# A six-sublayer network in one program: seams joined, a first unit issued ahead, the value bias folded away

## What is computed

```
x = x + 0.5 * ffn(_layernorm(x))      # 8 routed experts, top 2, and a shared one of width 1024
x = x + attn(_layernorm(x))           # gated linear attention, 4 heads, chunks of 16
x = x + 0.5 * ffn(_layernorm(x))      # the same experts again
x = x + 0.5 * ffn1(_layernorm(x))     # ternary weights, relu, width 1024
x = x + local(_layernorm(x))          # 16 heads of 16, window of 33 tokens
x = x + 0.5 * ffn1(_layernorm(x))
```

## Time and profile before

| what | value |
|---|---|
| time, median of 3 runs | 1747.06 us |
| lowest and highest | 1745.62 and 1749.57 us |
| profiled execution: time | 1750.36 us |
| its span, mean granted clock of TensorE | 1748.3 us, 0.984 |
| busy: PE, DVE, ACT, POOL | 94%, 65%, 49%, 39% |
| stages in the profile, us from the start of the span | first `ffn0` to 467, `gla` to 797, second `ffn0` to 1249, `l1ffn` to 1383, `win` to 1624, `l1ffn` to the end |

### The profile page before, as it was taken

The page is one execution under the profiler, slowest core; times in us unless marked ns, Lnnn a source line. Parts: engine busy times, 40 slices in busy tenths (PEclk is TensorE's granted clock), DMA queues, the critical chain, the costliest instruction groups (busy, mean ns, idle before and its releaser), DMA issues.

```text
span 1748.3 us, 42002 instructions
## 1 busy us (share of the span) xinstructions
PE 1650.5 (94%) x14972; PEld 1109.8 (63%) x14973; DVE 1142.2 (65%) x2498; ACT 857.5 (49%) x1475; POOL 682.4 (39%) x655
## 2 busy tenths in 40 slices
PE   6999999999989999989899999999799979998999
PEld 3565656666567767665555656666466657776666
DVE  6677766666466666657765556665577477777675
ACT  4355434443466566644344334443366455664764
POOL 2342323443122222132333324433244587887243
PEclk9999999999989999999999999999899999998999
DMA  7132323332211111003210123332332033131011
GB/s 251 49 108 83 106 74 103 109 111 91 52 38 36 24 24 24 1 1 94 85 38 34 39 67 111 110 112 83 80 67 42 1 75 74 40 76 39 14 36 48
DMA packets 90149, 115.82 MB, mean 66 GB/s; under 512 B 9296, under 2 KB 76400, under 8 KB 90032
## 3 DMA queue, kind: packets, MB, share of 16 engines
q1 hardware_dynamic: 68624, 70.25, 14.5%
q0 software_dynamic: 21408, 43.93, 9.0%
HBM read 66.24 MB, written 47.90 MB: 65 GB/s over the span
## 4 chain that ended last, share of the span: by engine, by line
PE 57%; DVE 6%; POOL 4%; ACT 3%; issue 2%; DMA 0%; DVEq 0%; SPq 0%; ACTq 0%; POOLq 0%
PE ps L1675 10%; PE ps L1677 10%; PE ps L1676 10%; PE ps L1909 3%; PE ps L1908 3%; PE ps L1691 2%; PE ps L2006 2%; PE ps L1890 2%; PE ps L1891 2%; PE ps L2163 2%; PE ps L2145 1%; PE ps L2011 1%; PE ps L2133 1%; POOL work L746 1%; PE ps L1970 1%
## 5 line engine op out<-in xcount | busy, mean ns | idle before, releaser
L703 POOL DMA_INDIRECT routed<-work x142 | 136.1, 959 | 234.9 <-DVE work L1431 229.8
L1675 PE MATMUL ps<-later_hi,work 128*128 (+1 forms) x632 | 203.2, 322 | 1.2 <-ACT work L1044 1.0
L1676 PE MATMUL ps<-later_lo,work 128*128 (+1 forms) x632 | 203.1, 321 | 0.0
L1677 PE MATMUL ps<-later_hi,work 128*128 (+1 forms) x632 | 203.0, 321 | 0.0
L1675 PE MATMUL ps<-xt_hi,wsh 128*128 128x512 f16 x512 | 194.9, 381 | 4.7 <-DVEq L1185 2.2
L1676 PE MATMUL ps<-xt_lo,wsh 128*128 128x512 f16 x512 | 194.9, 381 | 0.0
L1677 PE MATMUL ps<-xt_hi,wsh 128*128 128x512 f16 x512 | 194.8, 380 | 0.0
L640 POOL TENSOR_TENSOR rstd<-mv,eps 128x4 f32<-128x4 f32 x49 | 15.2, 309 | 409.1 <-DVE mv L1140 398.4
L854 ACT ACTIVATE work<-ps 128x512 f32<-128x512 f32 x128 | 76.4, 597 | 181.5 <-PE ps L1677 170.8
L1675 PE MATMUL ps<-wsh,work 128*128 128x256 f16 x512 | 140.7, 275 | 4.8 <-ACT work L843 2.7
L1324 DVE SCALAR_TENSOR_TENSOR work<-ps,work 128x512 f32<-128x512 f32 x128 | 88.1, 689 | 84.4 <-ACT work L854 69.1
(11 more groups left out here) (246 smaller groups left out, 4257.0 us busy)
## 6 DMA issues: line engine op xcount, KB each, us to landing
work<-expert_x SPq DMA_DIRECT2D x142, 129.0 KB
yg<-in_w_later SPq DMA_DIRECT2D x9, 496.0 KB
w1q<-in_w_later SPq DMA_DIRECT2D x9, 496.0 KB
yg<-routed SPq DMA_DIRECT2D x8, 512.0 KB, 3.7
yg<-routed POOLq DMA_DIRECT2D x8, 512.0 KB, 6.0
yg<-in_w SPq DMA_DIRECT2D x8, 512.0 KB
later_hi<-routed SPq DMA_DIRECT2D x8, 512.0 KB, 3.8
later_hi<-routed POOLq DMA_DIRECT2D x8, 512.0 KB, 5.9
```

The lines of the kernel that those rows point to most:

```text
L703: nc.gpsimd.indirect_dma_start(routed[:, :], bass.IndirectOffsetOnAxis(m.homes[:, i:i + 1], 0), m.t_y[:, i % 4, :], None).then_inc(s[f"til ...
L1675: nc.tensor.matmul(out_, a[0], b[0], start=start, stop=False)
L1676: nc.tensor.matmul(out_, a[0], b[1], start=False, stop=False)
L1677: return nc.tensor.matmul(out_, a[1], b[0], start=False, stop=stop)
```

## The change

**Behind the tiles (end of both `ffn0`).** Both routed rows of sequence 0 come by plain DMAs of SP into two free buffers (`opening_buffers`). DVE adds them to x in the middle of the last shared body (`combine_opening`, behind unit 4), and takes the statistics behind unit 6. The other operations of the chain move up too, and sequence 1 is combined and normed there, before the last `take`. PE transposes sequence 0 inside `down(0)`. The l1ffn behind it starts with sequence 1 normed (`AHEAD`), and `TURN_AT` is 4 in place of 2, in both `l1ffn`.

**Linear attention.** Its opening on DVE loses combine, statistics and scale of sequence 1. Its last body issues the first up unit of the next `ffn0` before `turn(0)`; the two pairs of banks of `up_bank` change places.

**Local attention.** The value bias isn't added to the values; since the weights of a softmax sum to 1, its product with the output weights is added to the output bias (`value_bias`, 6 matmuls, and one DVE operation), and the padding rows are filled with its negative. Sequence 1 is normed in the last part of `l1ffn` on DVE, and not by POOL; the two memsets of POOL move into `l1ffn`; the output bias of sequence g is added by POOL in step g. PE opens in another order.

**Elsewhere.** PE waits for `x_updated` before `gla` alone, and inside `l1ffn` before its first transposes. Loads at the start are a little smaller. The core of the diff:

```diff
-TURN_AT = 2
-AHEAD = ("win", )
+TURN_AT = 4
+AHEAD = ("ffn0", "win", )
...
+        def opening_buffers():
+
+            return xn[:, :, 0:D], ffn0_space().tile_x[:, :, 0:D]
...
         def up_bank(g, q):
 
-            return 2 * (q % 3) if is_last(g) else 2 + 2 * (q % 2)
+            return 2 * (q % 3) if is_last(g) else 4 - 2 * (q % 2)
...
+                for r in range(TOPK):
+                    sp.dma_start(opening_buffers()[r], routed_rows(0, r)).then_inc(s["opening"], 16)
                 buffers = yg_buffers(n + 1)
-                for q in range(NSEQ):
-                    if q >= len(buffers):
+                for q in range(1, NSEQ):
+                    if q > len(buffers):
                         sp.wait_ge(s["combined"], q + 1 - len(buffers) + G0)
...
+                    if ahead_of_win(n) and g >= NSEQ - 2:
+                        if g == NSEQ - 1:
+                            pool.wait_ge(S[n - 1]["combined"], 2 * NSEQ)
+                        nc.gpsimd.memset(win_space().vz[NSEQ - 1 - g], 0.0).then_inc(S[n + 1]["zeroed"], 1)
+                if ahead_of_win(n):
+                    rstd_of(N0(n + 1) + 1)
...
-                second_rows(n, 0)
-                rstd_of(N0(n + 1))
                 second_rows(n, 1)
+                for q in range(2):
+                    rstd_of(N0(n + 1) + q)
...
-                    if not is_last(g) and not second_last(g):
-                        output_bias(next_seq(g + 2))
+                    if is_first(g):
+                        pool.wait_ge(s["bias_row"], 1)
+                    output_bias(next_seq(g))
...
-                rstd_of(N0(n) + 1)
-                centre(N0(n) + 1, TPS)
-                scale(N0(n) + 1)
-                for q in range(2):
-                    output_bias(q * TPS)
-                nc.gpsimd.memset(m.vz[0], 0.0)
-                nc.gpsimd.memset(m.vz[1], 0.0).then_inc(s["zeroed"], 1)
...
+                nc.scalar.activation(m.bv[0], bv_col, ACT.Copy).then_inc(s["bias_hi"], 1)
                 queries_keys(0, 0, range(2 * KT))
-                nc.scalar.activation(m.sel[0:33, :], const("rowsel")[0:33, 0:1].broadcast_to([33, P]), ACT.Copy)
-                nc.scalar.activation(m.brow[0:33, :], rows[0:33, 2 * D:4 * D], ACT.Copy, scale=WS).then_inc(s["bias_hi"], 1)
+                xt_hi_of(N0(n) + 1, 1, WXT)
                 values_rows(0)
-                xt_hi_of(N0(n) + 1, 1, WXT)
                 windowed(act, step)
...
+            def combine_opening(n):
+
+                s = S[n]
+                first, second = opening_buffers()
+                dve.wait_ge(s["opening"], 32 * (1 + earlier(n)))
+                nc.vector.tensor_tensor(second, second, first, ALU.add).then_inc(s["opened"], 1)
+                dve.wait_ge(s["opened"], 1 + earlier(n))
+                nc.vector.tensor_tensor(x[:, 0:TPS, :], x[:, 0:TPS, :], second, ALU.add).then_inc(s["combined"], 1)
+                dve.wait_ge(s["combined"], 1 + earlier(n) * NSEQ)
                 dve.sem_inc(stood, 1)
...
+                        if is_last(g) and k == 4:
+                            combine_opening(n)
+                        if is_last(g) and k == 6:
+                            ln_stats(N0(n + 1), 0)
...
-                        combine(n, 0, 0)
-                        ln_stats(N0(n + 1), 0)
+                        ln_scale(N0(n + 1), 0)
+                        combine(n, 1, 1)
+                        ln_stats(N0(n + 1) + 1, TPS)
+                        xt_lo_of(N0(n + 1), 0)
...
                         ln_scale(g + N0(n) + 2, (g + 2) * TPS, into=m.xn[u])
                     take(0)
                     if is_last(g):
-                        ln_scale(N0(n + 1), 0)
-                        xt_lo_of(N0(n + 1), 0)
+                        ln_scale(N0(n + 1) + 1, TPS)
...
+                    if ahead_of_win(n) and is_last(g):
+                        ln_stats(N0(n + 1) + 1, TPS)
...
+                    if ahead_of_win(n) and is_last(g):
+                        ln_scale(N0(n + 1) + 1, TPS)
...
-                combine(n - 1, 1, 1)
-                ln_stats(N0(n) + 1, TPS)
-                ln_scale(N0(n) + 1, TPS)
...
+                        if t == 0 and is_first(g):
+                            ln_stats(N0(n) + 2, 2 * TPS)
+                            dve.wait_ge(s["bias_product"], 1)
+                            nc.vector.scalar_tensor_tensor(out=bo_row, in0=ps[:, 7, 0:D], scalar=1 / WS, in1=bo_row,
+                                                           op0=ALU.mult, op1=ALU.add).then_inc(s["bias_row"], 1)
...
+            def shared_unit(n, g, u, q):
+
+                b = up_bank(g, q)
+                for half in range(2):
+                    for k in range(KT):
+                        w = both((wsh1, wsh2)[half], slice(k * HSH + q * P, k * HSH + (q + 1) * P))
+                        ins = mm3(ps[:, b + half, :], w, xt(u, k), k == 0, k == KT - 1)
+                ins.then_inc(S[n]["up_ready"], 1)
+
+            def unit_ahead(n, g):
+
+                return is_first(g) and n > 0 and SUBLAYERS[n - 1] == "gla"
 
...
-                        up(q)
+                        if q or not unit_ahead(n, g):
+                            up(q)
...
-                        down(0)
-                        transposes(N0(n + 1))
+                        down(0, lambda: transposes(N0(n + 1)))
                         down(1)
...
                         if q == TURN_AT and is_first(g) and normed_ahead(n):
+                            pe.wait_ge(x_updated, N0(n))
                             transposes(N0(n) + 1)
...
+                    elif unit_ahead(n + 1, 0):
+                        xt_ready(N0(n + 1))
+                        gate_left(1)
+                        shared_unit(n + 1, 0, 0, 0)
                     turn(0)
...
-                def bias(half, at):
-                    nc.tensor.matmul(ps[:, half, :], m.sel[0:33, :], m.brow[0:33, None, at:at + D].broadcast_to([33, 2, D]),
-                                     start=True, stop=False, skip_group_check=True)
...
+                def value_bias():
+
+                    pe.wait_ge(s["bias_lo"], 1)
+                    for f in range(KT):
+                        own = tuple(b[:, f:f + 1].broadcast_to([P, P]) for b in m.bv)
+                        ins = mm3(ps[:, 7, 0:D], own, both(ao, slice(f * D, (f + 1) * D)), f == 0, f == KT - 1)
+                    ins.then_inc(s["bias_product"], 1)
...
-                        bias(half, D)
...
-                queries_keys(0, 0, range(2 * KT))
+                queries_keys(0, 0, range(KT))
+                transposes(N0(n) + 1, b=WXT)
+                queries_keys(0, 0, range(KT, 2 * KT))
+                scores(0, 0, 0)
                 values_rows(0, 0)
-                transposes(N0(n) + 1, b=WXT)
-                scores(0, 0, 0)
+                value_bias()
...
-                if n:
+                if kind == "gla":
                     pe.wait_ge(x_updated, N0(n))
```

More of the change, by code:

```diff
@@ L86 @@
 CONST_COLS = {"ident": 128, "ones": 128, "causal": 128, "cumref": 128, "tri": NE * NE,
-              "window": 64, "heads": 2, "heads_ws": 2, "rowsel": 1, "iota": TILES, "regions": NE,
+              "window": 64, "heads": 2, "heads_ws": 2, "iota": TILES, "regions": NE,
               "home": TOPK * NSEQ * TPS, "nowhere": TILES}
@@ L151, in build @@
         w2q = sb("w2q", [P, FU * D], F16)
-        rows = sb("rows", [P, 5 * D + NE])
+        rows = sb("rows", [P, 4 * D + NE])
         bgk_row, b2_row, bo_row = (rows[:, n * D:(n + 1) * D] for n in range(3))
-        bv_row = rows[:, 3 * D:5 * D]
-        ebias_row = rows[:, 5 * D:]
-        cols = sb("cols", [P, FU + 2 * KT + 1])
+        bv_row = rows[:, 3 * D:4 * D]
+        ebias_row = rows[:, 4 * D:]
+        cols = sb("cols", [P, FU + 3 * KT + 1])
         b1_col, bq_col, bk_col = cols[:, 0:FU], cols[:, FU:FU + KT], cols[:, FU + KT:FU + 2 * KT]
-        rms_col = cols[:, FU + 2 * KT:]
+        bv_col = cols[:, FU + 2 * KT:FU + 3 * KT]
+        rms_col = cols[:, FU + 3 * KT:]
         xn = sb("xn", [P, TPS, RW])
@@ L352, in back_by @@
         def back_by(n, q, odd):
-            return 8 * (q - odd) + 16 + 8 * NSEQ * earlier(n)
+            done = 16 * (NSEQ // 2 - (0 if odd else 1)) * earlier(n)
+            return 8 * (q - odd) + (16 if odd else 0) + done
         def yg_buffers(n):
@@ L432, in win_space @@
             m.hb = w([KT, 2])
-            m.brow, m.sel = w([2 * D], F16), w([P], F16)
+            m.bv = w([KT], F16), w([KT], F16)
             m.vrow = w([TPS, D])
@@ L824, in later_hi @@
                     act.wait_ge(ready0, 2)
-                    nc.scalar.activation(go[0][:], later_stage(odd, H * D), ACT.Copy, scale=rms_col).then_inc(later_hi_done, 1)
+                    nc.scalar.activation(go[0][:], later_stage(odd, H * D), ACT.Copy, scale=rms_col).then_inc(w_hi_done, 1)
                 else:
```

(11 more changed lines are left out.)

52 lines of the change are left out of this document (22 added, 30 removed).

## The result

The changed kernel takes 1716.88 us in the median of 4 runs (1716.48 to 1718.23), the kernel before 1747.84 (1745.62 to 1749.57): a ratio of 0.9825, 95% interval 0.9808 to 0.9842. That is 31.0 us less; 36.3 were forecast. Later, on one chip and beside each other, 5 runs gave 1715.97 against 1741.35 in 11 (0.985, 0.9837 to 0.9864), 25.4 us less. On two other chips the kernel before took 1748.57 and 1750.10 us (9 runs each), so it differs by 9 us with the chip. The chip of the first pair isn't on record, so whether 31.0 or 25.4 is nearer to what the change is worth stays open. The profiled execution has a span of 1714.4 us, 33.9 less than that of before, and a mean clock of 0.989.

The account below looks back on a forecast made before the run. PE, busy 94% of the span, was taken to set the time, with seams costing idle time and clock. Seven terms, 3.7 + 3.2 + 3.6 + 12.5 + 9.9 + 4.1 - 0.7, gave 36.3 us: 1710.7 from 1747.06, range 1703 to 1724.

Parts of the forecast that it names:

- First seam: From ffn0 to gla: the wait for the scale goes, transposes and down tile run at the high clock level; 3.7 us.
- Opening of linear attention: Keys' product starts when ACT's exponentials end, 1.85 us, plus half of the 2.76 lost by low clock, 1.35; sum 3.2.
- End of linear attention: A unit of 12 matmuls fills PE's wait before the turns and the x_updated wait goes; 3.6 us, bounds 2.5 and 4.7.
- Behind the second tiles: All four PE waits and the low clock go, less a new wait of 1.7; 12.5 us, bounds 9 and 13.5.
- Opening of local attention: POOL's first subtraction comes earlier, as sequence 1 is already normed; 9.9 us, bounds 8 and 11.
- Value bias: Bias matmuls leave PE's own path in six steps of local attention; 4.1 us, bounds 0 and 5.6.
- Last stage: TURN_AT of 4 loses 1.75 us against 1.05 from the earlier start; -0.7, bounds -1.2 and +0.5.
- seams only half closed: Rival, chance 0.25: VectorE has as much work, only in another order, so the seams give less; gain 27 us, 1720.
- Value bias beside the path: Rival, chance 0.07: the chain maximum, subtraction, exponential sets local attention's steps and covers PE's matmuls; gain 32.2 us, 1714.9.
- All levels come back: Rival, chance 0.11: the clock never falls in the openings; 1706.5 us.
- the swapped banks: Rival, chance 0.02: PE waits in each of 14 shared bodies for banks still read; a loss from 2.6 us a body on.

Follow-up runs that it names:

- combine_late: Changed kernel with the two adds and the statistics of sequence 0 behind the last low half of the last shared body, ahead of the scale; 1736.78 us in one run.
- bias_back: Changed kernel with a 128x512 matmul without use ahead of each half of the values in local attention; 1719.77 us in one run.
- turn2: Changed kernel with TURN_AT back at 2 in both l1ffn stages; 1715.27 us in 5 runs, ratio 0.9807.
- no_unit_ahead: Changed kernel without the up unit of ffn0 ahead of the last turn, and with the wait for x_updated back; 1725.94 us in one run.
- after_again: The changed kernel itself once more, unedited, on one chip beside others; median of 5 runs 1715.97 us, ratio to before 0.9850.
- turn2_again: Changed kernel with TURN_AT at 2 once more, on one chip beside others; median of 5 runs 1708.74 us, ratio to before 0.9810.
- best_again: Changed kernel with TURN_AT at 2, fillers in linear attention's opening, and second ffn0's statistics behind VectorE's first product, once more; 1711.35 us, ratio to before 0.9817.
- pool_load: Changed kernel with 20 additions without use on POOL ahead of its first subtraction in local attention; 1723.64 us in one run.

## Why the prediction was right, and where it was off

The time lies in its range, 6.2 us above the forecast (1710.7), and the waits went where it said. In part the number is luck: 3.3 of the 31.0 us are "the rest", for which it had nothing, and the pair on one chip has 25.4. By its own steps:

- *First seam*: right, 4.0 for 3.7. `combine_late` shows the cause; on its price see rstd above. The two adds and the statistics, costed at nothing, cost nothing here: PE has no wait from the last shared body's first product to the transposes.
- *Opening of linear attention*: the way to the first scores went from 22.08 to 20.39 us, 1.7 for 1.85. The clock gave 0.6 for 1.35. So the loss of 2.76 stayed nearly whole, and half of it was not a good guess: with fillers another 2.1 came.
- *End of linear attention*: 2.75 in the first pair of profiles, but eleven profiles with the unit have 108.3 to 112.2 us, 110.3 on the mean, against 112.5 and 112.8 in two of the order before. So it is some 2.3 and not 3.6; and 1.05 of the first pair's 2.75 is the wait for the routing, which I don't count to the change. VectorE now has both takes and the statistics ahead of its first product (790.46), so PE, in front, waits 0.59 us before the third unit, which takes the banks of the first.
- *Behind the second tiles*: 10.7 for 12.5. The step that was mis-sized is the new wait for the low half: 2.59 us for 1.7. The other 0.9 us lie in the six steps behind it, 94.51 us for 93.65: most steps there take 15.7 or 16.1 us, and how many take which varies from profile to profile. ScalarE has a relu and a high half in each unit and is the later engine here. Its rows, and VectorE's low half behind them:

```profile
1238.13 1.04 ACT L842 ACTIVATE xt_hi<-ps 128x1024 f16<-128x1024 f32 x1
1239.03 0.71 ACT L933 ACTIVATE work<-ps,cols 128x512 f32<-128x512 f32 x1
...
1239.60 0.66 ACT L926 ACTIVATE work<-work 128x512 f16<-128x512 f32 x1
1240.12 0.72 ACT L933 ACTIVATE work<-ps,cols 128x512 f32<-128x512 f32 x1
...
1240.29 0.69 DVE L1482 TENSOR_TENSOR work<-work 128x512 f16<-128x512 f32 x1 [1.32 <-ACT work L926]
1240.90 1.21 DVE L1164 TENSOR_TENSOR xt_lo<-ps,xt_hi 128x1024 f16<-128x1024 f32 x1
```

  A unit takes ScalarE 1.09 us (1239.03 to 1240.12) and PE 0.86 (four matmuls), so by unit 4 ScalarE is already behind by a unit: the transposes end at 1237.18, and their high half starts 0.95 us later. I had counted one pass through both engines and not this lag.
- *Opening of local attention*: right, 10.35 for 9.9, by order and load.
- *Value bias*: 2.85 for 4.1, and 3.2 by `bias_back`. I had charged the whole step to PE, with 0.1 on top for a broken rhythm that no run shows apart; and the 4.1 was added up wrongly, as 0.64 and 0.1 make 4.4 over six steps.
- *Last stage*: -2.4 for -0.7. Both priced parts were right: up to the first up unit 0.96 us are gained (1.05), and the turn costs 1.6 (1.75) while the level is kept. The mis-sized term is the clock behind the same 2.60 us wait, which the term left out, its lower bound being -1.2: 1.7 us. With the turn behind unit 4, stage L has 68.0 to 70.6 us in eight profiles of the changed kernel and its variants, and the first one is the longest.

Of the rivals, "seams only half closed" fell by its mechanism, since the waits went as the text said; by its number, 1720, it is nearer to 1716.9 than the forecast, and its 27 us lie between the 25.4 and the 31.0. "Value bias beside the path" fell by `bias_back`. "All levels come back" fell: the clock was 0.71, 0.91 and 0.79 in openings. The one of the swapped banks fell too, though not by A, whose body doesn't use the swapped pairs: in the first ffn0, from the transposes of the fourth sequence to those of the eighth, four bodies that do use them take 132.53 us in either kernel.

## What to carry to other kernels

Look at the engine behind the one that you relieve: moving the turn from unit 2 to unit 4 made a wait 2.2 us longer in each of two stages, because PE has less work left behind the turn and ScalarE comes to it later. And look at the next wait: in one of the stages it took back more than half, so the turn cost 0.9 us there and 1.5 in the other, and more only where the clock fell. Where a chain has a small operation on a third engine (rstd on POOL), count the two handovers, 1.5 us here. And measure a stage by marks within the program, in several profiles: gains of 2 to 3 us were plain there, and not in medians that differ by chip and by run; but a stage can have two lengths, and one profile shows only one of them.

## What was not expected of the hardware

The same wait keeps the clock in one execution and loses it in another. In the kernel before a wait of 2.70 us stood in a stretch at 1.00. In the first profile of `turn2` the same wait, in the same work, is followed by a lower one:

```profile
854.95 0.27 PE L1701 MATMUL ps<-wsh,work 128*128 128x256 f16 x1 [2.70 <-ACT work L853]
...
854.00:866.00 12.00, 10.67 (x87) 8.77 (x88) 9.03 (x24) 1.26 (x2) 1.48 (x3) 0.86 0.28 89
```

0.14 of 12 us is 1.7 us of the clock's, yet the stage hardly pays it. From the transposes of the third sequence to those of the fourth, around this wait, it takes 33.5 us in the four profiles that kept the level and 33.9 in nine of the ten that lost it. For in those four, and in no other, PE waits 1.07 us more for VectorE a little later, as in `no_unit_ahead`:

```profile
864.35 0.27 PE L1701 MATMUL ps<-wsh,work 128*128 128x256 f16 x1 [1.07 <-DVE work L1273]
```

Behind the turn there is no such wait, and there the loss counts in full, 1.4 to 1.7 us. So a seam that lost or kept its clock in one profile proves little, and what the loss costs is read from the wait behind it.

The wait for the routing of the second body, too, takes one of several lengths. In the kernel before and in the changed one, in the first ffn0:

```profile
52.11 0.19 PE L1717 MATMUL ps<-work,causal 128*128 128x32 f16 x1 [2.03 <-DVE work L1218]
```

```profile
50.91 0.19 PE L1756 MATMUL ps<-work,causal 128*128 128x32 f16 x1 [0.32 <-DVE work L1238]
```

This is 1.7 of the 3.3 us of "the rest", and I don't count it to the change: seven of its variants have 1.96 to 3.25 us there again, while the second profile of the changed kernel starts as quickly as its first. The lengths go with the chip. All four profiles of the chip of `after_again` (with `turn2_again`, `best_again` and `pool_load`) have 0.3 us there, and all eight of two other chips 1.9 to 3.3; in the second ffn0 it is 0.3 against 1.4 to 2.9. That the chip is the cause isn't shown: each of the three was used in one session only.
